# Decays of a state-space mixer: one exponential per chunk and head, later tokens hidden by GpSimd

## The chip, the core and the metric

The kernel runs on one core of a Trainium2 chip. The metric is its device time in microseconds. A core has five engines that run their own instruction streams in order and meet through semaphores: TensorE (PE), VectorE (DVE), ScalarE (ACT), GpSimd (POOL) and SyncE (SP), which here only issues transfers.

## What is computed

A layer norm, then a Mamba-2 style mixer over 4 sequences of 512 tokens with 64 heads of 64 channels in 8 groups, and beside it a small feed-forward branch of 4 streams with 50 Sinkhorn steps; the output is x + mixer * silu(branch). All in float32. The part that the change touches is the recurrence:

```python
dt_p = jax.nn.softplus(dt + dt_bias)
A = -jnp.exp(A_log)
dA = jnp.exp(dt_p * A)
dtx = dt_p[..., None] * x

def step(state, inp):
    dA_t, dtx_t, B_t, C_t = inp
    state = state * dA_t[..., None, None] + dtx_t[..., None] * B_t[:, :, None, :]
    y_t = jnp.einsum('bhpn,bhn->bhp', state, C_t)
    return (state, y_t)
```

The kernel has it in the form of an attention: y of token i is the sum over tokens j up to i of (C_i . B_j) * exp(cum_i - cum_j) * dtx_j, where cum is the running sum of dt_p * A. The log decays dt_p * A are at most zero, so cum falls with the tokens.

## The kernel before

Tokens come in two halves of 1024 (two sequences each). Within a half the kernel goes through the 8 groups, g = 0 to 7 and 8 to 15. Each group takes 20 slots s: slot s projects 128 channels over 512 tokens on TensorE (`project`, L1066 to L1071, 24 matmuls, since each float32 product is made from a high and a low part). Twelve slots feed the convolution (ScalarE's `tap`, L602, VectorE's three steps, L803, ScalarE's tanh, L610, VectorE's product to the SiLU, L815), eight feed the gate (L621, L622, L822). Each weight tile is split by ScalarE (w_hi, L586) and VectorE (w_lo, L785). A projection waits until the convolution of two slots before has read the same bank; `tap` of slot s waits, besides its projection, for the SiLU of slot s - 2.

Beside that a group has 8 units u, one for a pair of heads and a sequence q = u mod 2. A unit is a chain: SP loads, for both heads, a row of cum broadcast to all partitions (`load_cum`, L353) into one of three buffers (RING); ScalarE makes the decays in place (`exps`, L625 to L646); VectorE multiplies them with the scores (`weigh`, L841); TensorE multiplies with dtx (`mult`, L1107); VectorE adds D * x (`finish_y`, L863); ScalarE squares (`square`, L657); GpSimd adds the squares (L467) and gates y (L458). At the end of a group come, for each sequence q, a column sum on TensorE (L1117), a variance on VectorE (L871), a power on GpSimd (`rstd_of`, L473), a round trip of the result through memory to broadcast it (L362, L365), and the scaling of the gated output by GpSimd (`scale`, L481), stored at L368.

Keys j lie on the partitions, queries i on the columns. A sequence has four chunks of 128 keys; chunk k has the queries from its own start to the end, WIDTH 512, 384, 256 and 128 columns, at OFFSET 0, 512, 896, 1152; SPAN is 1280. Only the first 128 columns of a chunk (its own tokens) hold pairs whose query is earlier than the key; those are to give nothing.

In which slot of which group each step is issued stands in a table by hand, the `Plan` (L134 to L165): FIRST, LATER (six of eight groups in a half) and LAST. A unit's steps are placed around its mult slot: exponentials three and two slots before, weigh one before, square and gate one after, the tail of the group up to 7 slots after its last mult. A slot number of 20 and more falls into the next group's slots, and in each slot the older group's piece is issued ahead of the newer's (`open_groups`, L298). In LATER, exponentials of unit 0, head 0, stand in slot 6 and of head 1 in slot 7; of unit 1 in slots 8 and 9; the older group's variance and power of sequence 1 stand in slot 6 (26), its scalings in slots 7 and 9 (27 and 29), the second broadcast in slot 8 (28). SP issues the transfers in the same order, and the weight load of slot 8 waits until the w_lo of two tiles before is done.

In `exps` before, the 128 columns of a chunk's own tokens hold the row cum_i; Relu(cum_j - cum_i) is the fall, Exp(-fall) the decay, and pairs with a query earlier than the key come out as 1 and are removed by `masked` (L825 to L834), which multiplies the scores with a triangular mask when it takes them from the banks. The columns of later chunks hold a row that counts from the end of the key's chunk, and `dec` = total - cum_j is their bias; three `far` tables (L1006 to L1009) give those rows.

After the mixer comes the output stage (L1301 to L1303) with the Sinkhorn steps and the branch.

Of the kernel before, what the change touches and what calls it, by code (L numbers as in the profile page):

```python
# [19 lines left out]
ALU = mybir.AluOpType  # L20
# [3 lines left out]
P = 128  # L24
# [25 lines left out]
LOG_ZERO = -110.0  # L50

# [49 lines left out]
class Mixer:  # L101


    def __init__(self, nc, ctx):
# [25 lines left out]
        self.cum = sb("cum", [P, NT, HEADS])  # L130
        self.dec = sb("dec", [P, NT, HEADS])


class Plan:  # L134
# [3 lines left out]
    def __init__(self, cb, load, mult, gate_from, exp=None):  # L138
        self.cb, self.bc = cb, [s + 1 for s in cb]
        self.load, self.mult = load, mult  # L140
        self.exp = exp or [s - 3 + h for s in mult for h in range(2)]
        self.turn = [s - 2 for s in mult]
# [57 lines left out]
def mixer_programs(nc, ctx, core, mix, output):  # L200
# [49 lines left out]
    far = sums[:, 0, 0:3 * SEQS * HEADS].rearrange("p (a q h) -> p a q h", a=3, q=SEQS)  # L250
    cum_hm = bc[0:HEADS, :, :]
# [18 lines left out]
    fall_done, exp_done, cb_done, bc_done = sem("fall_done"), sem("exp_done"), sem("cb_done"), sem("bc_done")  # L270
# [180 lines left out]
    def run_gpsimd(pool):  # L451
# [16 lines left out]

        def rstd_of(g, q):

            pool.wait_ge(var_done, SEQS * g + q + 1)
            need(pool, rstd_stored[q], 16 * g)
            pool.tensor_tensor(rstd[:, q, :], var_eps[:, q, :], core.neg_half[:, 0:CHUNKS],  # L473
                               ALU.pow).then_inc(rstd_done, 1)
# [9 lines left out]
        def piece(g, plan, half, s):  # L484
            for u in due(plan.square, s):
# [95 lines left out]
    def run_scalar(act):  # L581
# [43 lines left out]
        def exps(g, at, u, h):  # L625
# [4 lines left out]
            if h == 0:  # L630
                act.wait_ge(cum_loaded[u % RING], 16 * (RING_USES[u % RING] * g + u // RING + 1))
            for k in range(CHUNKS):
                part = tile[:, OFFSET[k]:OFFSET[k] + P]
                op = act.activation(part, part, ACT.Relu, bias=mix.cum[:, CHUNKS * q + k, head], scale=-1.0)  # L634
            op.then_inc(fall_done, 1)
            for k in range(CHUNKS - 1):
                part = tile[:, OFFSET[k] + P:OFFSET[k] + WIDTH[k]]
                act.activation(part, part, ACT.Exp, bias=mix.dec[:, CHUNKS * q + k, head])  # L638
            act.wait_ge(fall_done, 2 * UNITS * g + 2 * u + h + 1)
            near = tile[:, 0:2 * WIDTH[0]].rearrange("p (a b) -> p a b", b=WIDTH[0])[:, :, 0:P]  # L640
            act.activation(near, near, ACT.Exp, scale=-1.0)
            step = WIDTH[2]
            near = tile[:, OFFSET[2] - P:OFFSET[2] - P + 2 * step].rearrange("p (a b) -> p a b", b=step)[:, :, P:step]
            op = act.activation(near, near, ACT.Exp, scale=-1.0)  # L644
# [1097 lines left out]
```

## Time and profile before

| | us |
|---|---|
| median of 3 runs | 3083.32 (3082.72 to 3083.66) |
| the profiled execution, its own time | 3077.91 |
| its span, first to last instruction | 3076.4 |

| engine | busy us | share of the span |
|---|---|---|
| TensorE, matmuls | 3006.5 | 98% |
| VectorE | 2177.6 | 71% |
| ScalarE | 1744.7 | 57% |
| GpSimd | 644.8 | 21% |

The page of the profile gives busy time by engine and the chain of work that ended last. A matmul record shows 0.39 us while the next one starts 0.23 us later: they overlap, so that a busy TensorE is one without gaps. In a view in order of time the columns are start in us, duration in us, engine, line, operation, output tile <- input tiles, shape, count; brackets at the end hold the idle time before it on its engine and what ended that. A transfer has the time of its issue in these views, not of its landing. "issue" as a cause means that the wait was for something the profile can't name.

### The profile page before, as it was taken

What the parts mean: (1) busy time and instruction counts of PE and PEld (TensorE: products, weight loads), DVE (VectorE), ACT (ScalarE), POOL (GpSimd) and SP (SyncE); (2) the same over time, 40 slices, a digit from 0 to 9 for tenths busy, and PEclk for the clock granted to TensorE, in tenths of its full rate; (3) what the DMA queues carried; (4) which work ended last, traced back from release to release, by engine and by line L of the source; (5) the groups of instructions that cost most, each with busy time, mean ns of one, the idle gap of its engine ahead of it and who ended that gap; (6) DMA issues with size and microseconds to landing.
All of it is one profiled execution on the core that took longest, in us unless ns stands there. A gap on an engine that the chain in (4) does not pass through costs nothing.

```text
span 3076.4 us, 45008 instructions
## 1 busy us (share of the span) xinstructions
PE 3006.5 (98%) x14304; PEld 2340.5 (76%) x14304; DVE 2177.6 (71%) x2660; ACT 1744.7 (57%) x3716; POOL 644.8 (21%) x447
## 2 busy tenths in 40 slices
PE   7999999999999998999999999999998999999998
PEld 6777777777777777777777777777776888887786
DVE  7667576676757687767676766767666878677877
ACT  3576575757566575576575757576675232234443
POOL 3322212121212234312222121222223000001112
PEclk9999999999999999999999999999999999999999
DMA  3434343333424353435243433334354444456665
GB/s 129 169 126 151 104 159 117 140 116 130 154 102 161 104 185 118 155 120 178 99 166 106 157 106 140 132 114 154 110 175 129 141 138 150 144 195 209 215 205 178
DMA packets 125528, 444.86 MB, mean 145 GB/s; under 512 B 17488, under 2 KB 21712, under 8 KB 109008
## 3 DMA queue, kind: packets, MB, share of 16 engines
q1 hardware_dynamic: 117552, 423.14, 41.0%
q0 software_dynamic: 4096, 14.68, 1.2%
q10 hardware_dynamic: 3744, 5.51, 0.5%
q8 instruction: 52, 0.85, 0.1%
q14 instruction: 84, 0.69, 0.1%
HBM read 397.86 MB, written 45.42 MB: 144 GB/s over the span
## 4 chain that ended last, share of the span: by engine, by line
PE 84%; DVE 6%; issue 6%; DMA 2%; ACT 2%; POOL 0%; SPq 0%; DVEq 0%; ACTq 0%; POOLq 0%
PE bank L1069 17%; PE bank L1071 17%; PE bank L1070 17%; PE bank L1107 8%; PE bank L1301 6%; PE bank L1302 6%; PE bank L1303 6%; PE bank L1081 2%; DVE acc L803 1%; PE bank L1093 1%; PE bank L1117 1%; DVE xbc L815 1%; DVE w_lo L785 1%; DMA acc<-in_w_out 1%; DMA units<-cum_scratch 1%
## 5 line engine op out<-in xcount | busy, mean ns | idle before, releaser
L1069 PE MATMUL bank<-x_hi,w_hi 128*128 128x512 f32 x2560 | 1023.9, 400 | 9.3 <-DVE acc L803 9.3
L1071 PE MATMUL bank<-x_hi,w_lo 128*128 128x512 f32 x2560 | 999.4, 390 | 0.0
L1070 PE MATMUL bank<-x_lo,w_hi 128*128 128x512 f32 x2560 | 997.3, 390 | 0.0
L803 DVE SCALAR_TENSOR_TENSOR acc<-bank,conv_w,acc 128x511 f32<-128x511 f32 (+2 forms) x576 | 430.7, 748 | 303.2 <-ACT acc L602 275.8
L1069 PEld LDWEIGHTS bank<-x_hi,w_hi 128*128 128x128 f32 x2560 | 480.6, 188 | 127.9 <-issue 23.1
L1071 PEld LDWEIGHTS bank<-x_hi,w_lo 128*128 128x128 f32 x2560 | 480.5, 188 | 104.2
L1070 PEld LDWEIGHTS bank<-x_lo,w_hi 128*128 128x128 f32 x2560 | 481.3, 188 | 93.6
L602 ACT ACTIVATE acc<-bank,tap_par 128x512 f32<-128x512 f32 x192 | 149.2, 777 | 579.7 <-PE bank L1071 434.1
L1301 PE MATMUL bank<-x_hi,w_hi 128*128 128x512 f32 x1024 | 402.5, 393 | 19.9 <-DVE x_lo L1293 15.6
L1302 PE MATMUL bank<-x_lo,w_hi 128*128 128x512 f32 x1024 | 400.4, 391 | 0.0
L1303 PE MATMUL bank<-x_hi,w_lo 128*128 128x512 f32 x1024 | 400.2, 391 | 0.0
L841 DVE TENSOR_TENSOR units<-units,bc 128x2560 f32<-128x2560 f32 x128 | 367.7, 2873 | 5.1 <-ACT units L644 5.1
L1285 ACT ACTIVATE w_hi<-w_raw 128x1024 fp32r<-128x1024 f32 x128 | 135.6, 1060 | 387.5 <-PE bank L1303 312.9
L638 ACT ACTIVATE units<-units,dec 128x384 f32<-128x384 f32 (+2 forms) x768 | 332.6, 500 | 0.0
L467 POOL TENSOR_TENSOR sums<-sums,sq 128x512 f32<-128x512 f32 x96 | 124.9, 1301 | 981.2 <-ACT sq L657 981.2
L634 ACT ACTIVATE units<-units,cum 128x128 f32<-128x128 f32 x1024 | 325.3, 394 | 9.0 <-DMA units<-cum_scratch 9.0
L785 DVE TENSOR_TENSOR w_lo<-w_raw,w_hi 128x1024 fp32r<-128x1024 f32 x160 | 203.3, 1271 | 156.9 <-ACT w_hi L586 156.9
L1107 PE MATMUL bank<-units,dtx 128*64 128x512 f32 (+3 forms) x2048 | 305.0, 440 | 3.6 <-DVE units L841 2.7
L822 DVE SCALAR_TENSOR_TENSOR gate<-th,gate 128x512 f32<-128x512 f32 x128 | 127.9, 1000 | 227.7 <-ACT gate L622 227.7
L458 POOL TENSOR_TENSOR gate<-gate,units 128x512 f32<-128x512 f32 x128 | 189.4, 1485 | 378.6 <-DVE gate L822 303.7
L1292 DVE TENSOR_TENSOR w_lo<-w_raw,w_hi 128x1024 fp32r<-128x1024 f32 x128 | 170.4, 1331 | 137.0 <-ACT x_hi L1286 136.6
L1107 PEld LDWEIGHTS bank<-units,dtx 128*64 128x64 f32 x2048 | 135.9, 137 | 168.7 <-issue 146.2
(154 smaller groups left out, 3388.2 us busy)
## 6 DMA issues: line engine op xcount, KB each, us to landing
units<-cum_scratch SPq DMA_DIRECT2D x128, 1280.0 KB, 6.8
w_raw<-in_w_in SPq DMA_DIRECT2D x160, 512.0 KB, 3.7
w_raw<-y_scratch SPq DMA_DIRECT2D x128, 512.0 KB, 3.6
y_scratch<-gate SPq DMA_DIRECT2D x32, 1024.0 KB, 6.6
acc<-in_w_out SPq DMA_DIRECT2D x128, 256.0 KB, 3.8
xbc<-in_x SPq DMA_DIRECT2D x16, 512.0 KB, 6.3
units<-in_x SPq DMA_DIRECT2D x16, 512.0 KB, 3.7
rstd_b<-rc_scratch SPq DMA_DIRECT2D x32, 256.0 KB, 4.1
```

The source lines that it names most:

```text
L634: op = act.activation(part, part, ACT.Relu, bias=mix.cum[:, CHUNKS * q + k, head], scale=-1.0)
L638: act.activation(part, part, ACT.Exp, bias=mix.dec[:, CHUNKS * q + k, head])
L785: dve.tensor_tensor(w_lo[m % 2][:, :, :], w_raw[:, m % 2, :, :], w_hi[m % 2][:, :, :].bitcast(F32), ALU.subtract).then_inc(w_split, 1)
L803: dve.scalar_tensor_tensor(acc[:, s % 2, back:], bank_proj[s % 2][:, 0:SEQ - back], mix.conv_w[:, at, m, 3 - back:4 - back], acc[:, s % 2, ...
L841: dve.tensor_tensor(attn[u % RING][:, :, :], attn[u % RING][:, :, :], bc[:, q, :].unsqueeze(1).to_broadcast([P, 2, SPAN]), ALU.mult).then_ ...
L1069: pe.matmul(out, w_hi[m % 2][:, k, :], hi, start=(k == 0), stop=False)
L1070: pe.matmul(out, w_hi[m % 2][:, k, :], lo, start=False, stop=False)
L1071: mm = pe.matmul(out, w_lo[m % 2][:, k, :], hi, start=False, stop=(k == KT - 1))
L1107: mm = pe.matmul(bank_y[u % 2][h * HD:(h + 1) * HD, k * P:SEQ], dtx[:, u % 2, k, h * HD:(h + 1) * HD], attn[u % RING][:, h, OFFSET[k]:OFFS ...
L1301: pe.matmul(self.bank[t][:, :], self.y_hi[j][:, toks], self.w_hi[j], start=first, stop=False)
L1302: pe.matmul(self.bank[t][:, :], self.y_hi[j][:, toks], self.w_lo[j], start=False, stop=False)
L1303: mm = pe.matmul(self.bank[t][:, :], self.y_lo[j][:, toks], self.w_hi[j], start=False, stop=last)
```

## The change

The row that is loaded now holds the fall from the key chunk's start to the query for every column (falls = -cum in the chunk, later chunks with the totals between added), so that one Exp with scale -1 and one bias, the key's own fall, serves a whole chunk: four activations per head in place of nine. Pairs with a query earlier than the key are set to 32768, a fall so large that its exponential is zero, by GpSimd: `hide`, four affine selects a unit, each over both heads' 128 columns, placed at the head of GpSimd's piece in the slot of the unit's first exponential. `hide` waits for the landing, ScalarE waits for `hide`. The scores are copied instead of multiplied with the mask. The far tables become six, made in three dependent steps; dec goes.

```diff
+NEVER = 32768.0
@@ Plan
+        self.hide = self.exp[0::2]
@@ run_gpsimd
+        def hide(g, u):
+            r = u % RING
+            pool.wait_ge(cum_loaded[r], 16 * (RING_USES[r] * g + u // RING + 1))
+            pool.nop(nofuse=True)
+            for k in range(CHUNKS):
+                near = attn[r][:, :, OFFSET[k]:OFFSET[k] + P]
+                op = pool.affine_select(out=near, in_=near, compare_op=ALU.is_ge, fill=NEVER, base=0,
+                                        pattern=[[0, 2], [1, P]], channel_multiplier=-1)
+            op.then_inc(hidden, 1)
...
         def piece(g, plan, half, s):
+            for u in due(plan.hide, s):
+                hide(g, u)
             for u in due(plan.square, s):
@@ exps
-            if h == 0:
-                act.wait_ge(cum_loaded[u % RING], 16 * (RING_USES[u % RING] * g + u // RING + 1))
+            act.wait_ge(hidden, UNITS * g + u + 1)
             for k in range(CHUNKS):
-                part = tile[:, OFFSET[k]:OFFSET[k] + P]
-                op = act.activation(part, part, ACT.Relu, bias=mix.cum[:, CHUNKS * q + k, head], scale=-1.0)
-            op.then_inc(fall_done, 1)
-            for k in range(CHUNKS - 1):
-                part = tile[:, OFFSET[k] + P:OFFSET[k] + WIDTH[k]]
-                act.activation(part, part, ACT.Exp, bias=mix.dec[:, CHUNKS * q + k, head])
-            act.wait_ge(fall_done, 2 * UNITS * g + 2 * u + h + 1)
-            near = tile[:, 0:2 * WIDTH[0]].rearrange("p (a b) -> p a b", b=WIDTH[0])[:, :, 0:P]
-            act.activation(near, near, ACT.Exp, scale=-1.0)
-            step = WIDTH[2]
-            near = tile[:, OFFSET[2] - P:OFFSET[2] - P + 2 * step].rearrange("p (a b) -> p a b", b=step)[:, :, P:step]
-            op = act.activation(near, near, ACT.Exp, scale=-1.0)
+                part = tile[:, OFFSET[k]:OFFSET[k] + WIDTH[k]]
+                op = act.activation(part, part, ACT.Exp, bias=mix.falls[:, CHUNKS * q + k, head], scale=-1.0)
@@ run_scalar, early
-                act.activation(mix.cum[:, :, :], by_head(bank_cum[:, :]), ACT.Copy).then_inc(e.cum_copied, 1)
+                act.activation(mix.falls[:, :, :], by_head(bank_cum[:, :]), ACT.Copy, scale=-1.0).then_inc(e.cum_copied, 1)
@@ masked, now scores_out
-                op = dve.tensor_tensor(bc[:, q, OFFSET[k]:OFFSET[k] + WIDTH[k]], cb_out[k],
-                                       core.mask[:, 0:WIDTH[k]], ALU.mult)
+                op = dve.tensor_copy(bc[:, q, OFFSET[k]:OFFSET[k] + WIDTH[k]], cb_out[k])
@@ run_vector, early
-                dve.tensor_tensor(far[:, 0], cum[:, :, 2, :], tot[:, :, 1, :], ALU.add).then_inc(e.far_step, 1)
-                dve.tensor_tensor(far[:, 1], cum[:, :, 3, :], tot[:, :, 2, :], ALU.add).then_inc(e.far_step, 1)
-                dve.wait_ge(e.far_step, 2)
-                dve.tensor_tensor(far[:, 2], far[:, 1], tot[:, :, 1, :], ALU.add).then_inc(e.far_step, 1)
-                dve.tensor_tensor(mix.dec[:, :, :], by_head(bank_tot[:, :]), mix.cum[:, :, :],
-                                  ALU.subtract).then_inc(e.far_step, 1)
+                for n in range(3):
+                    at = (0, 3, 5)[n]
+                    last = falls[:, :, 1:, :] if n == 0 else far[:, :, at - 3 + n:at, :]
+                    if n:
+                        dve.wait_ge(e.far_step, n)
+                    dve.tensor_tensor(far[:, :, at:at + 3 - n, :], last, tot[:, :, 0:3 - n, :],
+                                      ALU.subtract).then_inc(e.far_step, 1)
```

TensorE still makes ten transposes of the tables for each sequence.

## Rows read from the trace of the kernel before

**Rows 1.** The page: busy time by engine; the chain that ended last, by engine.
```profile
PE 3006.5 (98%) x14304; PEld 2340.5 (76%) x14304; DVE 2177.6 (71%) x2660; ACT 1744.7 (57%) x3716; POOL 644.8 (21%) x447
...
PE 84%; DVE 6%; issue 6%; DMA 2%; ACT 2%; POOL 0%; SPq 0%; DVEq 0%; ACTq 0%; POOLq 0%
```

**Rows 2.** Waits of TensorE: who for whom, us in total, times, longest.
```profile
PE bank L1301 <- DVE x_lo L1293: 15.6, 8, 7.0
PE bank L1069 <- DVE acc L803: 9.3, 16, 1.4
```

**Rows 3.** Order of time, group 6, ScalarE: decays of unit 0, next tap.
```profile
936.33 1.26 ACT L634 ACTIVATE units<-units,cum 128x128 f32<-128x128 f32 x4
...
939.00 0.40 ACT L644 ACTIVATE units<-units 128x256 f32<-128x256 f32 x1
942.76 0.78 ACT L602 ACTIVATE acc<-bank,tap_par 128x512 f32<-128x512 f32 x1 [3.36 <-PE bank L1071]
```

**Rows 4.** Order of time, group 6, GpSimd: all from 939 to 960 us.
```profile
939.34 1.01 POOL L473 TENSOR_TENSOR nrstd<-var_eps,neg_half 128x4 f32<-128x4 f32 x1 [11.79 <-DVE var_eps L871]
940.31 4.62 POOL L481 TENSOR_TENSOR gate<-gate,rstd_b 128x2048 f32<-128x2048 f32 x1
954.62 4.57 POOL L481 TENSOR_TENSOR gate<-gate,rstd_b 128x2048 f32<-128x2048 f32 x1 [9.70 <-DMA rstd_b<-rc_scratch]
```

**Rows 5.** Order of time, group 6, VectorE, slots 7 to 9.
```profile
943.58 2.32 DVE L803 SCALAR_TENSOR_TENSOR acc<-bank,conv_w,acc 128x511 f32<-128x511 f32 x3 [4.32 <-ACT acc L602]
...
948.60 1.22 DVE L785 TENSOR_TENSOR w_lo<-w_raw,w_hi 128x1024 fp32r<-128x1024 f32 x1
...
954.93 4.82 DVE L815 SCALAR_TENSOR_TENSOR xbc<-th,acc 128x512 f32<-128x512 f32 x1
960.65 2.32 DVE L803 SCALAR_TENSOR_TENSOR acc<-bank,conv_w,acc 128x511 f32<-128x511 f32 x3 [0.90 <-ACT acc L602]
```

**Rows 6.** Order of time, group 6, SyncE: issue of the second broadcast.
```profile
950.38 0.42 SPq L365 DMA_DIRECT2D rstd_b<-rc_scratch  x1
```

**Rows 7.** Order of time, group 6, TensorE: first matmul of slot 11.
```profile
963.02 0.50 PE L1069 MATMUL bank<-x_hi,w_hi 128*128 128x512 f32 x1 [0.52 <-DVE acc L803]
```

**Rows 8.** Order of time, group 15, VectorE and GpSimd at the same place.
```profile
2259.51 0.68 DVE L815 SCALAR_TENSOR_TENSOR xbc<-th,acc 128x512 f32<-128x512 f32 x1
...
2259.58 5.07 POOL L481 TENSOR_TENSOR gate<-gate,rstd_b 128x2048 f32<-128x2048 f32 x1 [10.17 <-DMA rstd_b<-rc_scratch]
```

**Rows 9.** Groups by line and shape: count, busy us, mean ns of one, idle before.
```profile
L634 ACT ACTIVATE units<-units,cum 128x128 f32<-128x128 f32 x1024 | 325.3, 394 | 9.0 <-DMA units<-cum_scratch 9.0
...
L638 ACT ACTIVATE units<-units,dec 128x384 f32<-128x384 f32 x256 | 155.3, 607 | 0.0
...
L641 ACT ACTIVATE units<-units 128x256 f32<-128x256 f32 x256 | 104.3, 407 | 0.0
```

**Rows 10.** Order of time, GpSimd, first 3 us: the two selects of the kernel before.
```profile
1.98 0.29 POOL L501 TENSOR_SCALAR_AFFINE_SELECT ident<-ident 128x128 f32<-128x128 f32 x1 [0.24 <-POOL neg_half L499]
2.24 0.61 POOL L503 TENSOR_SCALAR_AFFINE_SELECT mask<-mask 128x512 f32<-128x512 f32 x1
```

**Rows 11.** Order of time, group 7, ScalarE and GpSimd around unit 5.
```profile
1142.29 1.28 ACT L634 ACTIVATE units<-units,cum 128x128 f32<-128x128 f32 x4 [0.17 <-DMA units<-cum_scratch]
...
1143.48 2.69 POOL L511 TENSOR_SCALAR lv<-mv 128x1 f32<-128x1 f32 x1 [2.42 <-DVE mv L906]
```

**Rows 12.** Groups by line and shape: the mask product, widest form.
```profile
L832 DVE TENSOR_TENSOR bc<-bank,mask 128x512 f32<-128x512 f32 x32 | 21.9, 683 | 0.0
```

**Rows 13.** Order of time, group 8, TensorE: first transpose of the tables.
```profile
1249.32 0.41 PE L1198 MATMUL bank<-ident,cum 128*64 128x128 f32 x2 [1.34 <-DVE sums L1009]
```

**Rows 14.** Order of time, group 8, GpSimd and VectorE at 1227 us.
```profile
1226.78 1.28 POOL L558 TENSOR_TENSOR units<-units 128x512 f32<-128x512 f32 x1
1228.14 1.07 POOL L561 TENSOR_TENSOR units<-units 128x256 f32<-128x256 f32 x1
...
1226.87 1.74 DVE L815 SCALAR_TENSOR_TENSOR xbc<-th,acc 128x512 f32<-128x512 f32 x1
```

More of the change, by code:

```diff
@@ L129, in __init__ @@
         self.dt = sb("dt", [P, NT, HEADS])
-        self.cum = sb("cum", [P, NT, HEADS])
-        self.dec = sb("dec", [P, NT, HEADS])
+        self.falls = sb("falls", [P, NT, HEADS])
 class Plan:
@@ L249, in mixer_programs @@
     w_branch = sq[:, :].rearrange("p (k c) -> p k c", c=CW)
-    far = sums[:, 0, 0:3 * SEQS * HEADS].rearrange("p (a q h) -> p a q h", a=3, q=SEQS)
-    cum_hm = bc[0:HEADS, :, :]
+    far = flat(sums)[:, 0:6 * SEQS * HEADS].rearrange("p (q a h) -> p q a h", a=6, q=SEQS)
+    rows_hm = bc[0:HEADS, :, :]
     causal, ones, one = core.mask[:, 0:P], core.mask[:, P:2 * P], core.mask[:, SEQ - 1:SEQ]
@@ L269, in mixer_programs @@
     cum_loaded = [sem(f"cum_loaded{i}") for i in range(RING)]
-    fall_done, exp_done, cb_done, bc_done = sem("fall_done"), sem("exp_done"), sem("cb_done"), sem("bc_done")
+    hidden, exp_done, cb_done, bc_done = sem("hidden"), sem("exp_done"), sem("cb_done"), sem("bc_done")
     x_turned, dtx_done, attn_done, multiplied = sem("x_turned"), sem("dtx_done"), sem("attn_done"), sem("multiplied")
@@ L702, in early @@
                 act.wait_ge(e.cum_hm_copied, 3 * SEQS)
-                act.dma_start(d["cum"][half].rearrange("q h i -> h q i"), cum_hm).then_inc(e.cum_stored, 16)
+                act.dma_start(d["cum"][half].rearrange("q h i -> h q i"), rows_hm).then_inc(e.cum_stored, 16)
             t = s - EARLY_TURN - 1
@@ L823, in gate_silu, with scores_out @@
                                      gate[:, t, q * SEQ:(q + 1) * SEQ], ALU.add, ALU.mult).then_inc(gate_done, 1)
-        def masked(g, half, q, first):
+        def scores_out(g, half, q, first):
             dve.wait_ge(cb_done, SEQS * g + q + 1)
@@ L880, in piece @@
             for q in due(plan.bc, s):
-                masked(g, half, q, plan is FIRST)
+                scores_out(g, half, q, plan is FIRST)
             for u in due(plan.turn, s):
@@ L1001, in early @@
                 tot = bank_tot[:, :].rearrange("p (q k h) -> p q k h", q=SEQS, h=HEADS)
-                cum = mix.cum[:, :, :].rearrange("p (q k) h -> p q k h", q=SEQS)
+                falls = mix.falls[:, :, :].rearrange("p (q k) h -> p q k h", q=SEQS)
                 dve.wait_ge(e.summed, 2)
@@ L1193, in early @@
                 need(pe, e.cum_hm_copied, 3 * q)
-                near = [mix.cum[:, CHUNKS * q + k, :] for k in range(CHUNKS)]
-                ahead = [far[:, a, q, :] for a in range(3)]
-                for i, table in enumerate([near[0], near[1], ahead[0], ahead[2], near[1], near[2], ahead[1],
-                                           near[2], near[3], near[3]]):
+                near = [mix.falls[:, CHUNKS * q + k, :] for k in range(CHUNKS)]
+                ahead = [far[:, q, a, :] for a in range(6)]
+                for i, table in enumerate([near[0], ahead[0], ahead[3], ahead[5], near[1], ahead[1], ahead[4],
+                                           near[2], ahead[2], near[3]]):
                     mm = pe.transpose(bank_hm[i // 4][0:HEADS, (i % 4) * P:(i % 4 + 1) * P], table, core.ident[:, :])
```

2 lines of the change are left out of this document (1 added, 1 removed).

## The prediction

> **What bounds the kernel now.** I read the page first. TensorE is busy for 3006.5 of 3076.4 us at full clock, and its own work makes up 84% of the chain that ended last; ScalarE, which the change relieves most, is busy 57% [rows 1]. So a microsecond counts only where TensorE stands still. The list of waits, the second view, says where: the larger entries belong to the fronts of the halves and to the output stage (L1301, 15.6 us), and one comes from the loop, 9.3 us in 16 places, a projection (L1069) waiting for the convolution on VectorE (L803) [rows 2]. ScalarE's exponentials stand behind no entry of that list. The third view is the order of time in one group of the loop, g = 6, from 920 to 1058 us; the groups repeat it to a few tenths.
>
> There it reads like this. In slot 6 ScalarE makes the decays of unit 0, head 0, from 936.33 to 939.40 us, and the tap of slot 7 starts at 942.76, when TensorE delivers it: 3.4 us of slack [rows 3]. GpSimd finishes the power for sequence 1 of the group before at 940.35 (it waited 11.79 us for a variance that VectorE makes at the end of slot 6), scales sequence 0 until 944.93, waits for a transfer and scales sequence 1 from 954.62 to 959.20 [rows 4]. That transfer is issued at 950.38, behind a weight load that waits for the subtraction L785, which ends at 949.82 [rows 5, 6]. L785 stands in VectorE's order behind the convolution of slot 7 (943.58) with no idle time in between. Then the SiLU L815 starts at 954.93, 0.31 us after the second scaling, and takes 4.82 us where its usual time is 0.68: it ends when GpSimd ends, 0.55 later [rows 4, 5]. The tap of slot 9 waits for that SiLU, the convolution of slot 9 starts at 960.65, and TensorE, in need of it for slot 11, stands idle 0.52 us before 963.02 [rows 5, 7]. In group 15 the SiLU comes first by 0.07 us: it takes 0.68 us, the scaling pays, and TensorE doesn't wait [rows 8]. There are 12 such groups (2 to 7 and 10 to 15; 1 and 9 follow the FIRST plan); 11 lose this race.
>
> That chain has no slack: ScalarE's tap of slot 7, convolution, L785, transfer, scaling, SiLU, tap of slot 9, TensorE. What delays its start delays TensorE.
>
> **The change, part by part.** *ScalarE.* Removed per unit and head: four Relu of 128 columns (394 ns each), three far Exp (607 ns for 384 columns), two near Exp (407) [rows 9]. From the start of one row to the next, that head takes 3.0 us [rows 3]. Added: four Exp with a bias, of 512, 384, 256 and 128 columns. Two forms with a bias give the slope, (607 - 394) / 256 = 0.83 ns a column, and so 714 ns for 512; in the rows consecutive instructions start about 0.1 us before the one ahead has ended (four Relu in 1.26 us), so the four take 0.61 + 0.51 + 0.40 + 0.29 = 1.81 us. That frees 1.2 us a head, 300 us over 256 heads. I cost this gain at almost nothing, because TensorE's rows wait for it nowhere but in the last group (below).
>
> *GpSimd.* Added: four selects a unit, each 2 x 128 columns. The trace has two selects, 128 columns in 0.29 and 512 in 0.61 us [rows 10]; between them 256 columns give 0.39, four 1.55 us, with a wait and a nop 1.6. Bounds: 4 x 0.29 = 1.2 and 4 x 0.61 = 2.4 us. I take 1.6, the value between two rows of the same instruction. The Trainium skill (GPSIMD Engine Reference, section 3.1) gives 769 ns as measured for 512 elements in its best loop; by that price four selects come nearer to 2 us, and the sum below would rise by some 4 us.
>
> *Where the new wait stands.* GpSimd works in order. In slot 6 the older group's piece comes first, so hide(0) is queued behind the power of sequence 1 and starts at 940.3. The landing of unit 0's rows doesn't matter: ScalarE read them at 936.33. It ends at 941.9; ScalarE's first exponential starts at about 942.0 instead of 936.33. Queued behind it on ScalarE: 1.81 us of exponentials, then the tap of slot 7, at 943.8 instead of 942.76. That is 1.05 us late, and the chain above hands it on: convolution, SiLU of slot 6, L785, transfer, scaling and SiLU, since transfer and SiLU both count from L785 and the race stays as it is. The first scaling moves too, by 1.6 us, and hide(1) follows it at 946.5; a select can hold up the SiLU of slot 6 there by up to 0.4 us, I take 0.05. So 1.1 us for each of 11 groups: **+12.1 us**. With selects of 1.2 or 2.4 us it is 0.7 or 1.9 each, 8 or 21 us. In group 15 the wait lands in free time if it wins its race again.
>
> *Other hides of the loop.* Hide 1 follows the first scaling and is done by about 948.2, in slot 7, while ScalarE asks for it in slot 8; hide 2 follows the second scaling, with a slot and a half left. Hides 3 to 7 follow the landing of their rows, and there ScalarE had time: in all 1024 Relu it waited 9.0 us for landings [rows 9]. I cost them at nothing; without this cover each would cost up to 1.6 - 1.2 = 0.4 us, 24 us over the 60 of these units.
>
> *Groups 1 and 9.* After a FIRST plan sequence 0's power stands ahead of hide(0), not sequence 1's, and comes some microseconds earlier in the slot, so the tap is not late; selects may meet L785 twice, each time for up to one select. I take one, 0.4 us, in each: **+0.8**.
>
> *Group 7.* Here units 3, 4 and 5 were asked at the moment they landed, for unit 5 at 1142.29 [rows 11]. Now the selects come between, 1.6 against 1.2 us saved on the first head: I estimate 0.25 us at mult(2) and 0.8 at mult(4) (gate 0 now waits behind hide(4)). hide(5) also stands behind the statistics of the next half (L511, which took 2.69 us, to 1146.17), so unit 5 slips by up to 8 us; w_lo for slot 18 slips with it to about the time TensorE wants it, 0.5. Sum **+1.5**, between 0 and 4.
>
> *VectorE.* The mask product (L832, 683 ns for 512 columns) becomes a copy from the same bank [rows 12]; same shape, one input fewer, I cost it at 0, and up to 0.2 us less each would be hidden. At the start of each half TensorE stands 1.34 us waiting for the far tables [rows 13]. Three dependent steps of 384, 256 and 128 columns replace ones of 128: about 0.6 us more, twice: **+1.2**. The table dec goes, behind them.
>
> *End of the loop.* Before TensorE's waits at L1301 the last exponentials stand ahead of the w_hi of the output stage on ScalarE; the one that TensorE's delivery doesn't hold is 1.2 us shorter: **-1.2**.
>
> Sum 12.1 + 0.8 + 1.5 + 1.2 - 1.2 = 14.4 us: a span of 3090.8 after 3076.4, and 3092.3 for the profiled run after 3077.9. The median of the runs shown lies 5.4 above the profiled one, so the time predicted is 3083.3 + 14.4 = 3098.
>
> **Rivals.** *The SiLU wins its race.* If hide(1) or the landing moves the second scaling behind the SiLU by 0.3 us, each of 11 groups loses the 0.6 us stall and the tap's lateness disappears in some 4 us of room: -6.6 + 0.8 + 1.5 + 1.2 - 1.2 = -4.3, 3079. For it: group 15 shows it with 0.07 us. Against it: both sides count from L785, with margins of 0.2 to 0.3 us in the other groups. Chance 0.13.
>
> *Nothing is late.* If the wait in slot 6 is harmless (selects under 0.6 us in all, or an order on GpSimd that I misread) the sum is near 0 to -2, 3082; the ScalarE time gained then counts where I see nothing. This is also the case in which it could be faster by more than noise. Against it: one select alone takes 0.29 us. Chance 0.12.
>
> *Port blocking.* A SiLU that VectorE began at 1226.87, while a GpSimd instruction ran until 1228.06, ended at 1228.61, and GpSimd's next, begun at 1228.14, took 1.07 us [rows 14]: they block each other whole, and take turns. The change adds 512 selects that read SBUF. If selects went through back to back over a waiting VectorE instruction, the SiLU of slot 6 would wait for all of hide(1), 1.5 us more in each of 11 groups: +31, 3114. It decides from the point where a SiLU meets more than one select. The turns in the rows speak against it. Chance 0.1. The Trainium skill (SBUF — State Buffer, Who interferes with whom) says that a VectorE instruction with two SBUF inputs and a GpSimd instruction that reads SBUF exclude each other, the later one fully blocked; the trace agrees, 4.82 us for 0.68. By it alone these selects are a cost, never a help to VectorE.
>
> **Numbers.** The forecast has 0.65, with 3090 to 3107 as its own range. The range of 8 in 10 takes in the forecast with its bounds, the port case at its top and most of the harmless wait, and leaves the race case out: 3081 to 3114. A run of this kernel can tell about 0.2%, 6 us. Slower by more: the forecast and the port case, 0.76; within it: the race and the harmless wait, mostly, 0.17; faster by more: 0.07, the tails of these two.
>
> **What would show it.** ScalarE's first exponential of unit 0 at 942 instead of 936 in a group, released by GpSimd; the taps of slots 7 and 9 later by 1.1; TensorE's wait before slot 11 up from 0.5 to 1.7 us, in 11 groups. ScalarE's busy time down by 300, GpSimd's up by 200. Selects well over 0.4 us, or a SiLU of slot 7 at 0.68 us, would make it wrong.

## The result, and the profile after

The changed kernel takes 3106.0 us, median of 4 runs (3103.1 to 3108.6); the kernel before, on the same chip, 3083.0 (3082.4 to 3083.7). The ratio is 1.0074, with a 95% interval of 1.0057 to 1.0092: slower by 23 us. The forecast was 15 us slower, 3098, with 3081 to 3114 as the range. The profiled execution took 3108.6 us, span 3107.1, the highest of its four, where that of before took 3077.9, span 3076.4, near the low end of its kernel's (3076.9 to 3091.4 over this study); so the traces differ by 30.7 us where the medians differ by 23.

The page after: busy time by engine, the chain that ended last by engine, and three groups by line (TensorE's projection, ScalarE's exponentials, GpSimd's selects: busy us, mean ns of one, idle before and its releaser).

```profile
PE 3011.1 (97%) x14304; PEld 2344.3 (75%) x14304; DVE 2168.2 (70%) x2658; ACT 1448.1 (47%) x2436; POOL 938.6 (30%) x959
...
PE 17%; DVE 3%; issue 2%; DMA 2%; ACT 1%; POOL 1%; SPq 0%; DVEq 0%; ACTq 0%; POOLq 0%
...
L1073 PE MATMUL bank<-x_hi,w_hi 128*128 128x512 f32 x2560 | 1025.6, 401 | 23.8 <-DVE acc L807 23.8
...
L648 ACT ACTIVATE units<-units,falls 128x512 f32<-128x512 f32 (+3 forms) x1024 | 489.3, 553 | 188.2 <-POOL units L478 188.2
...
L478 POOL TENSOR_SCALAR_AFFINE_SELECT units<-units 128x256 f32<-128x256 f32 x512 | 301.0, 622 | 317.3 <-DMA units<-cum_scratch 317.3
```

ScalarE gave back the 300 us that were forecast (1744.7 to 1448.1, [rows 1]) and now stands 188 us waiting for selects. GpSimd took on 294, not 200. The chain of after is followed back only some way (its shares add to 26%), so it isn't compared with [rows 1]. The two rows to set beside [rows 2] are these, from the list of TensorE's waits (us in total, times, longest): the projection's wait for the convolution went from 9.3 to 23.8 us, and the wait of a transpose for `times_dt`, in one place, from 2.16 to 8.2 us.

```profile
PE bank L1073 <- DVE acc L807: 23.8, 17, 1.8
...
PE bank L1163 <- DVE dtx L853: 8.2, 1, 8.2
```

The same slots of group 6 in order of time, as [rows 3 to 7] show them of before. GpSimd, ScalarE, VectorE, SyncE, TensorE (start, us; in brackets the idle time before):

```profile
945.74 1.01 POOL L486 TENSOR_TENSOR nrstd<-var_eps,neg_half 128x4 f32<-128x4 f32 x1 [11.79 <-DVE var_eps L874]
946.71 1.48 POOL L478 TENSOR_SCALAR_AFFINE_SELECT units<-units 128x256 f32<-128x256 f32 x4
948.16 4.64 POOL L494 TENSOR_TENSOR gate<-gate,rstd_b 128x2048 f32<-128x2048 f32 x1
...
962.22 4.61 POOL L494 TENSOR_TENSOR gate<-gate,rstd_b 128x2048 f32<-128x2048 f32 x1 [7.54 <-DMA rstd_b<-rc_scratch]
...
948.32 1.92 ACT L648 ACTIVATE units<-units,falls 128x512 f32<-128x512 f32 x4 [5.49 <-POOL units L478]
950.15 0.76 ACT L617 ACTIVATE acc<-bank,tap_par 128x512 f32<-128x512 f32 x1
...
950.94 2.32 DVE L807 SCALAR_TENSOR_TENSOR acc<-bank,conv_w,acc 128x511 f32<-128x511 f32 x3 [5.28 <-ACT acc L617]
...
962.49 4.88 DVE L819 SCALAR_TENSOR_TENSOR xbc<-th,acc 128x512 f32<-128x512 f32 x1
968.28 2.32 DVE L807 SCALAR_TENSOR_TENSOR acc<-bank,conv_w,acc 128x511 f32<-128x511 f32 x3 [0.90 <-ACT acc L617]
...
957.95 0.42 SPq L366 DMA_DIRECT2D rstd_b<-rc_scratch  x1
...
970.65 0.50 PE L1073 MATMUL bank<-x_hi,w_hi 128*128 128x512 f32 x1 [1.75 <-DVE acc L807]
```

It reads as forecast. The four selects stand behind the power and take 1.48 us. ScalarE waits 5.49 us for them, and the tap of slot 7 starts at 950.15, 4.41 us after the power did; in before that distance was 942.76 - 939.34 = 3.42 us [rows 3, 4]. That lateness of 0.99 us goes through convolution, transfer, scaling and SiLU, and TensorE waits 1.75 us where it waited 0.52 [rows 7].

The difference by stretch, found by the start of the same matmul of TensorE in both traces, is as follows; columns are bounded by the times of the kernel before (us), and the same table is used for every experiment below, each against before.

| us later than before | 8-258 | 258-1010 | 1010-1378 | 1378-2191 | 2191-2394 | output | sum |
|---|---|---|---|---|---|---|---|
| what is there | front, groups 0, 1 | groups 2 to 6 | group 7, front of half 2 | groups 9 to 14 | group 15, end of loop | | |
| changed kernel | 0.6 | 6.9 | 9.9 | 5.0 | 8.0 | 0.3 | 30.7 |

So some 12 us are in the steady groups (2 to 6 and 10 to 14 for the most part), and 18 in the two places where a half ends. There is one profiled execution of each kernel. In the output stage, which no edit touches, the columns of this table and of those below lie between -3.1 and 3.1 us, so a single column is good to some 3 us at best.

The border of the halves in the trace of after: GpSimd, ScalarE, VectorE and TensorE.

```profile
1155.60 1.93 POOL L478 TENSOR_SCALAR_AFFINE_SELECT units<-units 128x256 f32<-128x256 f32 x4
...
1165.78 4.51 POOL L478 TENSOR_SCALAR_AFFINE_SELECT units<-units 128x256 f32<-128x256 f32 x4
...
1178.16 4.51 POOL L478 TENSOR_SCALAR_AFFINE_SELECT units<-units 128x256 f32<-128x256 f32 x4
...
1157.56 1.92 ACT L648 ACTIVATE units<-units,falls 128x512 f32<-128x512 f32 x4 [6.82 <-POOL units L478]
...
1170.33 1.92 ACT L648 ACTIVATE units<-units,falls 128x512 f32<-128x512 f32 x4 [5.06 <-POOL units L478]
...
1182.71 1.92 ACT L648 ACTIVATE units<-units,falls 128x512 f32<-128x512 f32 x4 [5.71 <-POOL units L478]
1184.53 0.57 ACT L636 ACTIVATE th<-bank 128x512 f32<-128x512 f32 x1
...
1179.39 3.02 DVE L844 TENSOR_TENSOR units<-units,bc 128x2560 f32<-128x2560 f32 x1
1185.71 0.69 DVE L826 SCALAR_TENSOR_TENSOR gate<-th,gate 128x512 f32<-128x512 f32 x1 [3.30 <-ACT gate L637]
1186.32 0.68 DVE L853 TENSOR_TENSOR dtx<-bank,dt 128x512 f32<-128x512 f32 x1
...
1187.06 1.97 PE L1163 MATMUL bank<-ident,xbc 128*128 128x128 f32 x8 [8.22 <-DVE dtx L853]
```

Three units in a row are late here. Two fours take 4.51 us instead of 1.48; the 3.03 us between are the length of one VectorE instruction that runs among them, the product of the scores with the decays (L844, 3.02 us). ScalarE is held 5 to 7 us by each four, its gate activations (L636, L637) stand behind the exponentials, VectorE's gate products (L826) behind them, and times_dt (L853) behind the gate products: TensorE stands 8.22 us at the first transpose of half 2. In before the same wait is for times_dt too, and is 2.16 us:

```profile
1171.24 1.61 PE L1159 MATMUL bank<-ident,xbc 128*128 128x128 f32 x8 [2.16 <-DVE dtx L850]
```

### The profile page after: what moved, and what is told of

Same layout as the page of the kernel before. It is cut to its first block and busy times, and to the rows that moved or that the text cites. A ratio compares the mean times of both kernels' runs of the same rounds, so it can differ in the third digit from the quotient of the medians.

```text
span 3107.1 us, 44298 instructions
## 1 busy us (share of the span) xinstructions
PE 3011.1 (97%) x14304; PEld 2344.3 (75%) x14304; DVE 2168.2 (70%) x2658; ACT 1448.1 (47%) x2436; POOL 938.6 (30%) x959
## 5 line engine op out<-in xcount | busy, mean ns | idle before, releaser
L1073 PE MATMUL bank<-x_hi,w_hi 128*128 128x512 f32 x2560 | 1025.6, 401 | 23.8 <-DVE acc L807 23.8
L1073 PEld LDWEIGHTS bank<-x_hi,w_hi 128*128 128x128 f32 x2560 | 481.3, 188 | 141.9 <-issue 27.6
L648 ACT ACTIVATE units<-units,falls 128x512 f32<-128x512 f32 (+3 forms) x1024 | 489.3, 553 | 188.2 <-POOL units L478 188.2
L478 POOL TENSOR_SCALAR_AFFINE_SELECT units<-units 128x256 f32<-128x256 f32 x512 | 301.0, 622 | 317.3 <-DMA units<-cum_scratch 317.3
L844 DVE TENSOR_TENSOR units<-units,bc 128x2560 f32<-128x2560 f32 x128 | 368.8, 2881 | 0.5 <-ACT units L648 0.5
L826 DVE SCALAR_TENSOR_TENSOR gate<-th,gate 128x512 f32<-128x512 f32 x128 | 113.3, 885 | 281.3 <-ACT gate L637 281.0
L1305 PEld LDWEIGHTS bank<-x_hi,w_hi 128*128 128x128 f32 x1024 | 194.1, 190 | 67.5 <-DVE x_lo L1297 20.9
```

The source lines that it names most:

```text
L478: op = pool.affine_select(out=near, in_=near, compare_op=ALU.is_ge, fill=NEVER, base=0, pattern=[[0, 2], [1, P]], channel_multiplier=-1)
L648: op = act.activation(part, part, ACT.Exp, bias=mix.falls[:, CHUNKS * q + k, head], scale=-1.0)
L844: dve.tensor_tensor(attn[u % RING][:, :, :], attn[u % RING][:, :, :], bc[:, q, :].unsqueeze(1).to_broadcast([P, 2, SPAN]), ALU.mult).then_ ...
L1073: pe.matmul(out, w_hi[m % 2][:, k, :], hi, start=(k == 0), stop=False)
L1305: pe.matmul(self.bank[t][:, :], self.y_hi[j][:, toks], self.w_hi[j], start=first, stop=False)
```

## The experiments

Theory T: the change costs by the places of its selects in GpSimd's in-order queue, and by ScalarE's waiting for them there. Rival R1: it costs by their work and their contention for the port, whether waited for or not. Rival R2: it costs by its other parts. Each kernel's ratio is to the kernel before on the same chip.

**No selects.**

```diff
-            for u in due(plan.hide, s):
-                hide(g, u)
...
-            act.wait_ge(hidden, UNITS * g + u + 1)
+            if h == 0:
+                act.wait_ge(cum_loaded[u % RING], 16 * (RING_USES[u % RING] * g + u // RING + 1))
...
-                op = act.activation(part, part, ACT.Exp, bias=mix.falls[:, CHUNKS * q + k, head], scale=-1.0)
+                op = act.activation(part, part, ACT.Exp, bias=core.neg_half[:, 0:1], scale=-1.0)
```

> This is the changed kernel without its selects; ScalarE waits for the load alone, as in the kernel before, and the exponentials take a constant bias of -0.5, so that nothing grows without bound. Left out of the computation: pairs with a later token are not hidden and the decay within a chunk is not the reference's. The work of ScalarE, VectorE and TensorE stays that of the changed kernel. Theory T (the cost of the change is the selects and their places in GpSimd's queue): all of the 23 us goes, 3082 us, within 3. Rival R2 (the cost is in the other parts: the far tables, the copies of the scores, the longer single exponentials): at least half of it stays, 3094 us or more.

Measured: 3074.2 us, ratio 0.9970 (0.9959 to 0.9981). R2 falls: the other parts don't cost, they gain 9 us on before. T's figure was 8 us too high; it gave ScalarE's relief no value. The traces show some relief: 0.2 us in each steady group, and 1.4 in group 7, where an attention product of TensorE waited 1.34 us for VectorE's product with the decays and no longer does. Another 1.6 us at the border is not relief: there the trace of before has 3.4 us at the lower clock level behind a wait of 2.16 us, and this one has the same wait and no such stretch. The traces differ by 4 us where the medians differ by 9, because the profiled execution of before is 5 us under the median of its kernel.

**Selects that nobody waits for.** ScalarE as in the last kernel; `hide` is back at its old places, but works on a spare tile `spot` of the same shape, each select waiting, besides the landing, only for the one before the last:

```diff
             for k in range(CHUNKS):
-                near = attn[r][:, :, OFFSET[k]:OFFSET[k] + P]
-                op = pool.affine_select(out=near, in_=near, ...)
-            op.then_inc(hidden, 1)
+                pool.wait_ge(hidden, CHUNKS * (UNITS * g + u) + k + 1)
+                pool.nop(nofuse=True)
+                pool.affine_select(out=spot[:, k % 2], in_=spot[:, k % 2], ...).then_inc(hidden, 1)
```

> The kernel without waits on selects (as the first of these four, with the same parts of the computation left out), but GpSimd does all 512 selects at their old places on an unrelated tile of the same shape, and no engine waits for them. Theory T: GpSimd's own later steps (power, scaling) come later by up to 1.5 us, but nobody's exponentials wait; the group keeps at most half of its 1.0 us, 3083 to 3090 us. Rival R1 (the selects cost by their work and at the port, not by being waited for): 3098 us or more.

Measured: 3080.4 us, ratio 0.9992 (0.9981 to 1.0003). In that kernel's page:

```profile
L480 POOL TENSOR_SCALAR_AFFINE_SELECT spot<-spot 128x256 f32<-128x256 f32 x512 | 306.3, 632 | 304.2 <-DMA units<-cum_scratch 304.0
```

All the work is there, 306 us, and it costs 6 us over no selects (0.9992 against 0.9970). The wait for them costs the other 26 of the 32 us that lie between no selects and the changed kernel; R1 is a fifth of it. Being blocked matters only through the wait: at the border the fours are stretched here too, and TensorE's wait for `times_dt` there is 2.16 us, as in before.

```profile
1164.81 4.53 POOL L480 TENSOR_SCALAR_AFFINE_SELECT spot<-spot 128x256 f32<-128x256 f32 x4
```

In the table:

| us later than before | 8-258 | 258-1010 | 1010-1378 | 1378-2191 | 2191-2394 | output | sum |
|---|---|---|---|---|---|---|---|
| no selects | 0.5 | -0.9 | -2.5 | -1.0 | 0.2 | -0.2 | -4.0 |
| selects, no wait | 0.5 | 2.0 | -2.4 | 1.3 | 1.1 | -1.8 | 0.6 |

**First four one slot earlier**, ahead of the older group's power.

```diff
-        self.hide = self.exp[0::2]
+        self.hide = [self.exp[0] - (mult[0] == 9)] + self.exp[2::2]
```

> The changed kernel with one edit: the first four selects of a group are issued one slot earlier, ahead of the older group's power and scaling, in all groups but the first of a half. Theory T (ScalarE's exponentials and its tap of slot 7 wait for selects that stand behind the older group's power): the ten steady groups lose about 1.0 us each and group 15 about 1.6, so some 3094 us (3091 to 3097). Rival R1 (the sum of select time on GpSimd and at the port costs the time, wherever the selects stand): 3106 us, within 3.

Measured: 3092.9 us, ratio 1.0030 (1.0018 to 1.0042), 13 us less than the changed kernel, as T said. The steady groups are as quick as before, -0.5 and -1.8 in the columns for them; the border keeps its 9.4 us and the end 5.2.

**Also the last three fours ahead of the statistics.** Units 5, 6 and 7 of the last group of a half are issued one slot earlier, behind the slot's own squares and gate products.

```diff
+        self.hide_end = []
+        if exp:
+            self.hide_end = [self.hide.pop() - 1 for _ in range(3)][::-1]
...
                 for group in open_groups(g, s, half, plan, before):
                     piece(*group)
+                for u in due(plan.hide_end, s):
+                    hide(g, len(plan.hide) + u)
```

> The changed kernel with the first four selects of a group one slot earlier, and in the last group of a half also the last three fours one slot earlier, ahead of the next half's statistics. Theory T: the 1.0 us of each steady group goes, and most of the 8 us at the border of the halves and of the 4.7 us at the end of the loop: 3083 to 3088 us. Rival R1 (work and port): 3106 us, within 3. A rival of half a step (only the steady groups react, the border is due to the statistics' own lateness): 3094 us.

Measured: 3089.0 us, ratio 1.0020 (1.0011 to 1.0030). T's 3083 to 3088 was too hopeful, and R1's 3106 is far off: 6.5 us stay at the border and 6.0 at the end. TensorE's wait is now

```profile
1175.72 1.54 PE L1168 MATMUL bank<-ident,xbc 128*128 128x128 f32 x6 [5.64 <-DVE dtx L858]
```

and GpSimd's fours there still meet VectorE, whatever stands ahead of them:

```profile
1144.65 4.14 POOL L481 TENSOR_SCALAR_AFFINE_SELECT units<-units 128x256 f32<-128x256 f32 x4 [2.69 <-DMA units<-cum_scratch]
...
1157.06 4.51 POOL L481 TENSOR_SCALAR_AFFINE_SELECT units<-units 128x256 f32<-128x256 f32 x4
```

**The same three fours at the head of the slot**, the first four one slot earlier as in the last two.

```diff
+        if exp:
+            self.hide[5:] = [s - 1 for s in self.hide[5:]]
```

> The changed kernel with the first four selects of a group one slot earlier, and in the last group of a half the fours of units 5, 6 and 7 one slot earlier and at the head of the slot, ahead also of its squares and gate products. In the version that put them behind the piece the border of the halves was still 6.0 us and the end of the loop 6.0 us later than in the kernel before, with single waits of TensorE of 5.64 and 1.33 us there. Theory T (place in the queue): half of these 12 us goes, 3083 to 3086 us. Rival R1 (in these two groups VectorE and GpSimd hold each other up, so a four takes 4 us wherever it stands): 3089 us, within 2.

Measured: 3095.6 us, ratio 1.0039 (1.0026 to 1.0051): both sides missed, it is worse. The border is at 8.0 us, the end at 9.3. Its rows:

```profile
1145.30 1.48 POOL L480 TENSOR_SCALAR_AFFINE_SELECT units<-units 128x256 f32<-128x256 f32 x4 [10.62 <-DMA units<-cum_scratch]
1146.75 1.30 POOL L470 TENSOR_TENSOR sums<-sums,sq 128x512 f32<-128x512 f32 x1
...
1154.35 4.53 PE L1113 MATMUL bank<-units,dtx 128*64 128x512 f32 x16 [5.71 <-DVE units L846]
```

This four isn't blocked (1.48 us), and the transposes wait 2.16 us as in before. But it stands at the head of the queue 10.62 us for rows that haven't landed, with the square and the gate product behind it. The 5.7 us have moved from the border's transposes to an attention product. So at the border every place tried costs: late behind the statistics, blocked behind the products, or holding them up.

**Eight selects of 128x128 for four of 128x256.**

```diff
             for k in range(CHUNKS):
-                near = attn[r][:, :, OFFSET[k]:OFFSET[k] + P]
-                op = pool.affine_select(...)
+                for h in range(2):
+                    near = attn[r][:, h, OFFSET[k]:OFFSET[k] + P]
+                    op = pool.affine_select(...)
```

> The changed kernel with eight selects of 128x128 in place of each four of 128x256. By the select of 0.29 us that the kernel before shows, eight take 2.3 us against 1.48, 0.8 us more. T (the price of a unit's selects is passed on to TensorE where ScalarE waits for them): about 12 groups give 0.8 us each, and the border and the end of the loop three units of 0.8 us each: 15 us more than the changed kernel, 3121 us (3115 to 3127). R1 (work and port, no wait): the increase has no favoured place; by GpSimd's 105 us of added time it would be in proportion to the 23 us for 301 us, 8 us, 3114 us. If the selects' price doesn't matter: 3106 us.

Measured: 3137.9 us, ratio 1.0176 (1.0159 to 1.0193). The direction is T's, the size above everyone's. Eight take 2.01 us in group 6, 0.53 more than four and not 0.8, and TensorE's wait at slot 11 there is 2.34 us, 0.6 more. But in other groups a second stop appears, for VectorE's product of the scores with the decays. The three rows:

```profile
955.83 2.01 POOL L479 TENSOR_SCALAR_AFFINE_SELECT units<-units 128x128 f32<-128x128 f32 x8
...
980.38 0.50 PE L1074 MATMUL bank<-x_hi,w_hi 128*128 128x512 f32 x1 [2.34 <-DVE acc L808]
...
828.40 1.94 PE L1112 MATMUL bank<-units,dtx 128*64 128x512 f32 x10 [1.17 <-DVE units L845]
```

And behind the longer waits TensorE's clock falls in seven of the twelve groups 2 to 7 and 10 to 15, where it fell in one of the changed kernel; the last section prices such a stretch at 1.7 us. In the table the columns of groups 2 to 6 and 9 to 14 are at 18.1 and 13.3 us, 11.2 and 8.3 more than the changed kernel, for selects that are 0.5 us longer in each. So the delay is passed on one for one, and beyond that it is paid again, by a second chain whose slack it uses up and by the clock.

**Each scaling in two instructions.** The wait in the steady groups ends with a SiLU held for a whole scaling, so the scaling was cut, first in the kernel before:

```diff
-            pool.tensor_tensor(part, part, rstd_b[:, q, :].unsqueeze(1).to_broadcast([P, XT, SEQ]),
-                               ALU.mult).then_inc(scaled, 1)
+            for c in range(0, XT, 2):
+                op = pool.tensor_tensor(part[:, c:c + 2], part[:, c:c + 2],
+                                        rstd_b[:, q, :].unsqueeze(1).to_broadcast([P, 2, SEQ]), ALU.mult)
+            op.then_inc(scaled, 1)
```

> The kernel before, with each scaling on GpSimd cut into two instructions of half the size and nothing else. T2: its own waits of 0.52 us in 11 groups go, 3077 us (3075 to 3079). Rival: 3083 us, within 2.

Measured: 3060.5 us, ratio 0.9930 (0.9911 to 0.9948). It beats both kernels, and by 17 us more than T2 said. VectorE and GpSimd in group 6:

```profile
949.39 2.60 DVE L817 SCALAR_TENSOR_TENSOR xbc<-th,acc 128x512 f32<-128x512 f32 x1
...
949.08 5.19 POOL L482 TENSOR_TENSOR gate<-gate,rstd_b 128x1024 f32<-128x1024 f32 x2 [9.54 <-DMA rstd_b<-rc_scratch]
```

The SiLU is held until the first half ends, 2.60 us for 4.82 [rows 5]. TensorE's waits for the convolution fall from 9.3 us in 16 places [rows 2] to 0.8 in 2.

**The same cut in the changed kernel**, its selects left where they are:

> The changed kernel, its selects at their places, with each scaling on GpSimd cut into two instructions of half the size. Theory T (a late first four delays the chain that ends in the SiLU behind the scaling, and costs nothing where that chain has room): the SiLU is held some 2.3 us less, which is more than the 1.75 us that TensorE waits at slot 10 in a steady group, so the selects of the steady groups cost nothing; the kernel keeps only the border of the halves and the end of the loop over the kernel before with the same cut (3060.5 us): 3106 less 11 groups of 2.05 us is 3083 us, within 4. Rival (the selects cost their 1.0 us in each steady group whatever else waits): 3106 - 25 + 0 is no better than the gain of the kernel before, and more exactly the steady groups stay 1.0 us behind: 3094 us or more.

Measured: 3076.1 us, ratio 0.9975 (0.9964 to 0.9986), 30 us less than the changed kernel, and 7 less than T's 3083. The rival's 3094 is off by far more. This is the cleanest test of the chain. The selects are as late as ever, but TensorE doesn't notice:

```profile
936.31 1.48 POOL L478 TENSOR_SCALAR_AFFINE_SELECT units<-units 128x256 f32<-128x256 f32 x4
...
937.92 1.92 ACT L650 ACTIVATE units<-units,falls 128x512 f32<-128x512 f32 x4 [5.49 <-POOL units L478]
...
951.90 2.63 DVE L821 SCALAR_TENSOR_TENSOR xbc<-th,acc 128x512 f32<-128x512 f32 x1
...
PE bank L1075 <- DVE acc L809: 0.8, 2, 0.6
```

ScalarE still waits 5.49 us. The steady groups are within 0.6 us, in all, of the kernel before with the same cut (table below). The rival, that selects cost their microsecond in any case, falls. T's number was off because the cut gained at the ends of the halves too, where T left the changed kernel as it was: 9.9 to 4.8 us and 8.0 to 1.0 in the table.

**With the cut and the better places.** The first four of a group is one slot earlier in both. The last three fours stand at the head of the slot in the first, and behind the slot's products in the second:

> The kernel of the run above with each scaling of 128x2048 numbers on GpSimd cut into two instructions of half the size. Theory T2 (the SiLU that stands ahead of slot 9's convolution starts while the scaling runs and is held for 4.9 us; that is TensorE's 0.6 us wait in every steady group): the SiLU is held for 2.5 us at most, the wait of 0.6 us goes in 11 groups, 6 us less than the run above, 3078 to 3080 us. Rival (the second half of the scaling holds the next VectorE instruction just the same): no change against the run above, within 2.

Measured: 3075.3 us, ratio 0.9968 (0.9956 to 0.9981), 3 us under T2's 3078 to 3080 and 20 us under the same kernel without the cut; the rival falls.

> The version with the first four selects one slot earlier and the last three fours behind the piece but ahead of the statistics, with each scaling cut into two. T: that version took 3089 us; the cut took 20 to 25 us from both kernels that it was tried in, so 3067 us (3064 to 3071), still behind the kernel before with the same cut (3060.5 us), by the border and the end of the loop. Rival (with the cut the change as a whole pays off, since ScalarE has 300 us less to do): 3058 us or less.

Measured: 3071.4 us, ratio 0.9965 (0.9953 to 0.9978), just above T's 3064 to 3071; the rival, 3058 us or less, falls. By their ratios this and the last kernel can't be told apart, and both stay behind the kernel before with the same cut. This one does so by 0.0035, 11 us. By the traces 12, of which 5 are at the border and 6 in the output stage, where no row was followed.

| us later than before | 8-258 | 258-1010 | 1010-1378 | 1378-2191 | 2191-2394 | output | sum |
|---|---|---|---|---|---|---|---|
| before, scaling in two | -0.3 | -6.2 | -3.5 | -6.6 | 1.6 | -3.1 | -18.2 |
| changed, scaling in two | 1.0 | -6.0 | 4.8 | -6.2 | 1.0 | 0.0 | -5.4 |
| the same, last fours behind the products | 1.0 | -6.2 | 1.4 | -6.5 | 1.2 | 3.1 | -6.1 |

**Before, scaling in four instructions.**

> The kernel before with each scaling cut into four instructions of 128x512. T2 (in the cut into two no steady group of TensorE waits any more): nothing is left to win there, 3060 us, within 3. Rival (each further cut shortens the hold of VectorE and shows at the border and the end): 3055 us or less. If the extra instructions themselves cost: above 3064 us.

Measured: 3060.1 us, ratio 0.9931 (0.9912 to 0.9949): the same as in two. Nothing is left to win in the steady groups.

## Why the prediction was right, and where it was not

*Right, and shown by rows.* The bound, and the chain from the tap of slot 7 to TensorE at slot 11. The selects' price: 1.48 us, and with the wait and the nop 1.6, as taken between the two rows of the same instruction [rows 10]. The Trainium skill (GPSIMD Engine Reference, section 3.1) gives 769 ns for 512 elements in its best loop. In proportion, an estimate from that page, the 1024 columns of a four take 1.54 us. The unblocked fours agree with that, though 512 columns in one select took 0.61 us [rows 10]; the prediction's "nearer to 2 us" doesn't follow from the page's figure alone. The tap late by 0.99 for 1.05 us, TensorE's wait 1.75 for 1.7. The steady groups cost 11.4 us for groups 2 to 6 and 10 to 14, and group 7 has its own microsecond in the border's account: +12.1 held, with 1.7 us of the clock in one of the ten (last section). ScalarE's -300 held too. The far tables cost 1.05 for 1.2, groups 1 and 9 cost 0.5 for 0.8. That it was this chain, and not the selects' work, is shown by three interventions: the first four earlier, selects without a wait, and the SiLU's hold shortened.

*The term that failed: the ends of the halves.* "Group 7, +1.5, between 0 and 4", and "End of the loop, -1.2". Measured: group 7 and the border 9.9 us with the next front's tables, 8.06 of them at the last transposes of half 1 and the first of half 2; the end 4.7 and group 15 3.3 us. The clock has a part in it: 0.9 of the 8.06 us, and some 1.6 of the 4.7 (last section). Two steps of the argument were wrong. The first said that hides 3 to 7 follow the landing of their rows; for units 5 to 7 they follow the statistics and gate products in GpSimd's queue. The prediction saw hide(5) slip by up to 8 us, and priced only the weight w_lo that slips with it. It didn't follow the lateness on through ScalarE's gate activations, VectorE's gate products and times_dt, nor to units 6 and 7. The second took a four as 1.6 us everywhere. In the steady groups that holds; here the four meets VectorE's product of 3.0 us, and took 4.51 us twice at the border (4.51 and 5.50 at the end). The mean select took 622 ns, and that is also why GpSimd got 294 us more and not 200.

*The term that was left out: ScalarE's relief.* It was costed at almost nothing, 1.2 us in all, since "ScalarE's exponentials stand behind no entry of that list". That reading missed an entry: VectorE's product with the decays (L841) works on what they make, TensorE waited 2.7 us for it in three places of before, and in the kernel without selects the longest of these, 1.34 us in group 7, is gone. By the medians that kernel is 9 us ahead of before, by the traces 4. So by the medians the selects cost 32 us and not some 15, and the rest of the change, this relief above all, gave 9 back. That the sum came as near as it did is in part luck.

*The race.* The prediction costed group 15 at nothing, if it won its race again. It lost:

```profile
2282.65 4.97 DVE L819 SCALAR_TENSOR_TENSOR xbc<-th,acc 128x512 f32<-128x512 f32 x1
...
2282.47 4.60 POOL L494 TENSOR_TENSOR gate<-gate,rstd_b 128x2048 f32<-128x2048 f32 x1 [7.41 <-DMA rstd_b<-rc_scratch]
...
2290.98 0.47 PE L1073 MATMUL bank<-x_hi,w_hi 128*128 128x512 f32 x1 [1.35 <-DVE acc L807]
...
2312.63 1.72 PE L1111 MATMUL bank<-units,dtx 128*64 128x512 f32 x8 [1.56 <-DVE units L844]
```

A margin of 0.07 us [rows 8] should not have been costed at nothing; it is lost without selects too, where TensorE waits 0.57 us in that place. With the second stop, of 1.56 us, 3.3 us came from this group.

*The rivals.* "The SiLU wins its race" and "nothing is late" didn't occur. "Port blocking" was stated as back-to-back selects holding VectorE, 1.5 us in each of 11 groups and 31 us in all; it didn't occur (in group 6 the SiLU of slot 6 took 0.88 us for 0.68). What occurred at the border is its mirror: VectorE and GpSimd in turns, so that four short selects pay for one long VectorE instruction.

*The sum.* For the profiled execution 14.4 us were forecast and 30.7 measured, so the sum was half of it. Against the medians it looks better, 15 and 23, for the reason given under the result; which of the columns holds the 8 us by which the traces differ more isn't known. The verdict and the range held; the size of the term in the steady groups held; the places that repeat only twice held the error.

*Open.* Which share of the border's 8 us is the late statistics and which the blocked selects wasn't separated: each shift of the selects changed both. And part of the kernel before's gain by the cut, 22 us by the ratio and 25 by the medians, isn't in the steady groups. Its trace shows 18 us: 12.8 in the two columns for them, 3.5 in the column of group 7 and the border, of which 0.9 is group 7's own stop and the rest wasn't followed, and 3.1 in the output stage. The rest is about the 5 us by which before's profiled execution is under the median of its kernel.

## What to carry to other kernels

Where an engine works in order, the place of a new instruction is its price: the same 512 selects cost 6 us when nobody waited and 32 when somebody did, and nothing in the steady groups once the chain behind them had 2 us of room. When a part is relieved by moving work to an idle engine, follow the lateness through every engine that waits, above all at the few places where two phases share a queue; they are short and easy to cost at nothing. And look for the long instruction that holds a short one on the critical chain: cutting it in two gave 0.7%, as much as the change under study took.

## What the runs showed of the hardware

*A stop costs TensorE more than the listed wait.* In group 6 of before the last matmul ahead of the wait starts at 962.11 and the next at 963.02, where matmuls otherwise start 0.23 us apart: 0.68 lost for a wait of 0.52, and 0.11 more until the second start. So 0.27 us came on top of this stop. A group had two (the second of 0.08 us); if that one had the same addition, which wasn't read, the two make 0.79 + 0.35 = 1.1 us, and the cut scaling gained 1.05 a group.

*The clock falls after a wait, but not each time.* In one steady group of after the wait was 1.80 us:

```profile
546.03 0.50 PE L1073 MATMUL bank<-x_hi,w_hi 128*128 128x512 f32 x1 [1.80 <-DVE acc L807]
...
547.74 0.63 PE L1073 MATMUL bank<-x_hi,w_hi 128*128 128x512 f32 x1
548.17 0.63 PE L1074 MATMUL bank<-x_lo,w_hi 128*128 128x512 f32 x1
...
550.94 0.39 PE L1075 MATMUL bank<-x_hi,w_lo 128*128 128x512 f32 x1
```

From 547.3 to 550.7 matmuls start 0.43 us apart where they otherwise start 0.23 apart, the lower of the two clock levels, and that costs 1.7 us. The other steady groups of after show no such stretch, though one of them waits 1.85 us, and neither does any steady group of before, with waits of 0.5 to 0.65 us, or of the kernels with the cut scaling, with none. With eight selects seven of twelve groups show one, behind waits of 2.27 to 2.51 us, and others with waits of 2.23 to 2.31 us show none. At the ends of the halves the trace of after has more of it than before. From 1182.1, within the stop of 8.22 us, its clock is at the lower level for 10.2 us, where before has 3.4, and that adds 0.9 us. At 2370.0 it has 3.4 us more, behind a wait of 3.39 us, where before waits 3.20 us and its clock stays. In all the clock makes some 4 of the 30.7 us between the two traces.

*Selects.* A select of 128x256 takes 0.37 us when four run back to back, and eight of 128x128 take 2.01, 0.25 each. From the two, an estimate: 0.12 us for 128 columns, and 0.13 us for each instruction.
